# A four-layer attention kernel on one Trainium2 core: row maxima transposed before they are split, and the layer norm's pieces spread between them

## The reference, cut to what matters

```python
x = L0_attn_a_x                                             # (16, 512, 256), fp32
x = x + _L0_attn_a_ref(_layernorm(x, axis=-1), ...)         # causal
x = x + _L0_ffn_ref(_layernorm(x, axis=-1), ...)            # split
x = x + _L0_attn_b_ref(_layernorm(x, axis=-1), ...)         # rotary
x = x + _L0_ffn_ref(_layernorm(x, axis=-1), ...)            # split
# inside each: scores = q k^T / sqrt(16); attn = softmax(scores); out = attn v; out @ Wo
```

## Time and profile before

| what | value |
|---|---|
| median of 3 runs | 4944.91 us (4940.63 to 4948.76) |
| the profiled execution: its own time | 4945.49 us |
| the profiled execution: span of its trace | 4943.7 us |
| mean granted TensorE clock in the span | 0.974 |
| PE busy | 4445.3 us, 90% |
| DVE busy | 3209.4 us, 65% |
| ACT busy | 2548.2 us, 52% |
| POOL busy | 1656.7 us, 34% |

### The profile page before, as it was taken

How to read it: one execution, slowest core, us unless ns; L and a number is a source line. 1 busy time by engine, 2 the same in 40 slices (tenths; PEclk the granted TensorE clock), 3 DMA queues, 4 the chain that set the end, 5 groups by cost and what they waited for, 6 DMA issues and landing times.

```text
span 4943.7 us, 70632 instructions
## 1 busy us (share of the span) xinstructions
PE 4445.3 (90%) x26116; PEld 1877.8 (38%) x26116; DVE 3209.4 (65%) x6576; ACT 2548.2 (52%) x3362; POOL 1656.7 (34%) x922
## 2 busy tenths in 40 slices
PE   4899999999969999899898999999999699999998
PEld 2454545454423333333333333333333233333333
DVE  4555555555447776767676676676676277777776
ACT  1444444444425555555455555555555255666565
POOL 2354545454432344352534334334324400000000
PEclk8999999999979999999999999999999799999999
DMA  4453535344322333423333334334333133333331
GB/s 131 122 155 118 156 114 156 124 150 127 107 89 82 92 114 96 114 83 113 99 96 112 98 113 120 96 106 120 98 104 120 54 86 90 89 89 90 91 89 44
DMA packets 302406, 525.36 MB, mean 106 GB/s; under 512 B 58348, under 2 KB 236272, under 8 KB 285680
## 3 DMA queue, kind: packets, MB, share of 16 engines
q1 hardware_dynamic: 259568, 485.19, 33.7%
q10 hardware_dynamic: 42496, 35.66, 2.2%
HBM read 317.10 MB, written 201.46 MB: 105 GB/s over the span
## 4 chain that ended last, share of the span: by engine, by line
PE 71%; DVE 17%; DMA 6%; issue 3%; ACT 3%; POOL 1%; DVEq 0%; ACTq 0%; SPq 0%; POOLq 0%
PE o_ps L1249 17%; PE scores L1197 16%; PE scores_t L1228 11%; DVE neg_max L864 10%; PE turn_ps L1277 10%; DMA q_stack<-shift_rows 5%; PE turn_ps L1324 5%; PE turn_ps L1284 4%; PE turn_ps L1255 4%; DVE bn L822 2%; DVE xn L839 2%; PE turn_ps L1289 1%; DVE shift_parts L874 1%; PE scores L1200 1%; PE scores L1212 1%
## 5 line engine op out<-in xcount | busy, mean ns | idle before, releaser
L864 DVE TENSOR_REDUCE neg_max<-scores 128x1 f32<-128x512 f32 (+3 forms) x4096 | 2489.2, 636 | 1285.9 <-PE scores L1197 760.0
L1065 ACT ACTIVATE probs<-scores_t 128x1024 f32<-128x1024 f32 (+2 forms) x2048 | 1926.3, 947 | 1484.8 <-PE scores_t L1228 1007.3
L1197 PE MATMUL scores<-k_stack,q_stack 98*128 98x512 bf16 (+4 forms) x4096 | 1428.3, 371 | 239.6 <-DVE neg_max L864 179.5
L1228 PE MATMUL scores_t<-q_stack,k_stack 100*128 100x512 bf16 (+3 forms) x4096 | 1187.5, 364 | 59.2 <-DMA q_stack<-shift_rows 58.3
L1249 PE MATMUL o_ps<-probs,values 128*32 128x512 f32 (+1 forms) x8192 | 1021.4, 571 | 0.2 <-ACT probs L1065 0.2
L1197 PEld LDWEIGHTS scores<-k_stack,q_stack 96*128 96x128 bf16 (+1 forms) x4096 | 396.7, 97 | 1635.8 <-DVE neg_max L864 1209.1
L1228 PEld LDWEIGHTS scores_t<-q_stack,k_stack 100*128 100x128 bf16 x4096 | 378.4, 99 | 380.5 <-issue 137.7
L725 POOL TENSOR_TENSOR parts<-qk_f,parts 128x1024 bf16<-128x1024 f32 x128 | 272.6, 2130 | 660.3 <-ACT parts L1105 491.1
L745 POOL TENSOR_TENSOR sim_inv<-sim_parts,minus_half 128x64 f32<-128x64 f32 x32 | 337.7, 10552 | 249.9 <-DVE sim_parts L946 249.9
L738 POOL TENSOR_TENSOR x_res<-x_res,o_bias_s 128x1024 f32<-128x1024 f32 x32 | 75.6, 2362 | 956.8 <-DMA x_res<-x_after 956.8
L696 POOL TENSOR_SCALAR var_eps<-mean_var 128x4 f32<-128x4 f32 x64 | 14.7, 230 | 978.6 <-DVE mean_var L828 978.6
(11 more groups left out here) (117 smaller groups left out, 4035.2 us busy)
## 6 DMA issues: line engine op xcount, KB each, us to landing
q_stack<-q_parts SPq DMA_DIRECT2D x1536, 64.0 KB, 2.6
values<-v_stage SPq DMA_DIRECT2D x64, 1024.0 KB, 4.2
values<-values SPq DMA_DIRECT2D x64, 1024.0 KB, 6.2
k_parts<-parts SPq DMA_DIRECT2D x192, 256.0 KB, 2.7
q_parts<-parts SPq DMA_DIRECT2D x192, 256.0 KB, 3.3
k_stack<-k_parts SPq DMA_DIRECT2D x256, 192.0 KB, 3.2
k_stack<-k_parts SPq DMA_DIRECT2D x256, 128.0 KB, 3.2
x_after<-x_res ACTq DMA_DIRECT2D x48, 512.0 KB, 2.9
```

The costliest lines, as they stand in the source:

```text
L864: nc.vector.tensor_reduce(neg_max[:, h % G, t:t + 1], bank[:, 0:n], AX.X, ALU.max, negate=True).then_inc(max_done.sem, 1)
L1065: nc.scalar.activation(probs[c][:, h % G, 0:n], st[i][:, 0:n], ACT.Exp).then_inc(exp_done.sem, 1)
L1197: last = nc.tensor.matmul(bank[:, 0:n], q[0:r, h, t * P:(t + 1) * P], k[0:r, h, 0:n], start=True, stop=kind != CAUSAL)
L1228: last = nc.tensor.matmul(st[i][:, off:off + L - q0], k[0:ROWS, h, kt * P:(kt + 1) * P], q[0:ROWS, h, q0:L], start=True, stop=kind != CAUSAL)
```

## The change

Three things are changed.

1. The maxima are not split before the transpose. PE transposes the 16 columns of `neg_max` as fp32 (16 by 128 in PSUM); DVE then makes the high part by a cast from PSUM and the low part by a subtraction whose first operand is in PSUM and whose second is the high part in SBUF. `shift` and `shift_parts` are gone. `neg_max` has two halves, used by groups in turn.
2. ACT issues two transfers for a group, one for each row of `q_stack`, from 16 partitions each.
3. Statistics and normalisation are cut into single pieces, one behind each maximum: the next stage's statistics at (slot, tile) (6,0), (6,2), (6,3), (7,0), the four BN_AGGR at (7,1), the normalisation at (8,0) to (8,3). The later batch's are at (9,0) to (9,3), (10,0), and (11,0) to (11,3).

```diff
-NXT_STATS_AT = (6, 1)
-NXT_NORMALISE_AT = (8, 0)
-X_STATS_AT = (8, 1)
-X_NORMALISE_AT = (10, 1)
+NXT_STATS_AT = {(6, 0): 0, (6, 2): 1, (6, 3): 2, (7, 0): 3, (7, 1): T}
+NXT_NORMALISE_AT = {(8, t): t for t in range(T)}
+X_STATS_AT = {(9, 0): 0, (9, 1): 1, (9, 2): 2, (9, 3): 3, (10, 0): T}
+X_NORMALISE_AT = {(11, t): t for t in range(T)}
...
-        neg_max = sb("neg_max", [P, G, T])
-        shift_parts = sb("shift_parts", [P, 2, G * T], BF16)
-        shift_rows = sb("shift_rows", [2 * G * T, P], BF16)
+        neg_max = sb("neg_max", [P, 2, G, T])
+        shift_rows = sb("shift_rows", [G * T, 2, P], BF16)
...
             def maximum(B, h, t):
                 kind = STAGES[B.s]
 
-                if h % G == 0 and t == 0 and (h or not B.first):
-                    shift_ready.wait(dve, B + (0 if h else -1), (h // G - 1) % NG)
+                g = h // G
+                if h % G == 0 and t == 0 and (g >= 2 or not B.first):
+
+                    turn_full.wait(dve, B + (0 if g >= 2 else -1), "sh", (g - 2) % NG)
...
-            def shift(B, g):
-
-                dve.wait_ge(max_done.sem, max_done.after(B, G * g + G - 1, T - 1))
-
-                if g or not B.first:
-                    turn_full.wait(dve, B + (0 if g else -1), "sh", (g - 1) % NG)
-                nm = neg_max[:, :, :].rearrange("p h t -> p (h t)")
-                nc.vector.tensor_copy(shift_parts[:, 0, :], nm).then_inc(shift_high.sem, 1)
-                dve.wait_ge(shift_high.sem, shift_high.after(B, g))
-                nc.vector.tensor_tensor(shift_parts[:, 1, :], nm, shift_parts[:, 0, :],
-                                        ALU.subtract).then_inc(shift_ready.sem, 1)
...
-                    nc.vector.tensor_copy(shift_rows[:, :], turn_b[0:2 * G * T, :]).then_inc(turn_free.sem, 1)
+                    rows = turn_ps[0:G * T, 0:P]
+                    nc.vector.tensor_copy(shift_rows[:, 0, :], rows).then_inc(shift_high.sem, 1)
+                    dve.wait_ge(shift_high.sem, shift_high.after(B, i))
+                    nc.vector.tensor_tensor(shift_rows[:, 1, :], rows, shift_rows[:, 0, :],
+                                            ALU.subtract).then_inc(turn_free.sem, 1)
...
-                act.dma_start(q_stack[B.n % 2][SHIFT:SHIFT + 2, G * g:G * g + G, :],
-                              shift_rows[:, :]).then_inc(shift_in.sem, 16)
+                for a in range(2):
+                    act.dma_start(q_stack[B.n % 2][SHIFT + a:SHIFT + a + 1, G * g:G * g + G, :],
+                                  shift_rows[:, a, :]).then_inc(shift_in.sem, 16)
...
                 elif k == "sh":
-                    pe.wait_ge(shift_ready.sem, shift_ready.after(B, i))
+                    pe.wait_ge(max_done.sem, max_done.after(B, G * i + G - 1, T - 1))
...
                 elif k == "sh":
-                    last = nc.tensor.transpose(turn_b[0:2 * G * T, :],
-                                               shift_parts[:, :, :].rearrange("p a c -> p (a c)"), ident_b[:, :])
+                    last = nc.tensor.transpose(turn_ps[0:G * T, 0:P],
+                                               neg_max[:, i % 2, :, :].rearrange("p h t -> p (h t)"), ident[:, :])
```

104 lines of the change are left out of this document (52 added, 52 removed).

## The result

| what | before | after |
|---|---|---|
| median of 4 runs | 4946.84 us | 5061.16 us (5046.37 to 5072.54) |
| ratio, 95% interval | | 1.0228 (1.0195 to 1.0262) |
| the profiled execution: time, span | 4945.49, 4943.7 us | 5054.6, 5052.8 us |
| mean granted clock | 0.974 | 0.967 |
| PE busy | 4445.3 us | 4496.3 us |

What follows compares the result with a forecast made beforehand. PE was taken to set the end, standing where it waits for DVE's maxima, statistics and normalisation and for the shift's transfer. Terms -66 - 55 - 40 + 22 + 15 + 0 = -124 from 4945.5 us gave 4820, range 4755 to 4900.

Steps and rivals of the forecast that it cites:

- Stalls behind POOL: Shift instructions with both ends in SBUF, which wait for POOL, are removed, mainly in the split stage's slot 2: -66 us.
- Single pieces: Statistics and normalisation between maxima in slots 6 to 11 hold PE up less: -55 us, between 15 and 91 gained.
- The pair in slots 1, 5, 9, 13 is gone: Without DVE's split ahead of the transpose, 0.5 us returns in 80 slots of the later stages: -40 us.
- The fp32 transpose: Each of PE's 256 shift transposes takes 0.28 us instead of 0.23: +15 us with the longer weight load.
- The pair behind the transpose: Cast and subtraction, 0.4 us longer than one copy, delay the first maximum of slots 3, 7, 11, 15: +22 us.
- Two transfers: Landing of the shift's rows: later and earlier effects of two requests cancel: 0 us, between -50 and +75.
- "earlier" side: For the rows' landing: a shorter issue, 0.42 us for 0.62, and 0.65 us less queueing bring 0.85 us.
- "later" side: For the rows' landing: 0.4 us for DVE and 0.42 for the second issue delay it by 0.82 us.
- "Slower": Rival: both transfers queue like the worst seen, one behind the other, rows landing 2.5 us later: 5070 us, chance 0.05.
- The gain of about 35 us: By the skill's rule a one-row transfer runs on 16 engines instead of 2, making the time about 35 us lower.

Runs made afterwards that it cites:

- a_runs: The changed kernel with one three-row transfer in place of two of one row, and statistics and normalisation in runs as before; 5019 us, ratio 1.0128.
- b_ kernels: Variants of the kernel before; the five meant keep its old cast and subtraction and edit only transfers or SP's store; 4870 to 5111 us.
- b_pieces: The kernel before with only statistics and normalisation cut into single pieces between the maxima; 4870 us, ratio 0.9833.
- b_two: The kernel before with only the transfer changed: two transfers of one row in place of one of two rows; 5111 us, ratio 1.0327.
- a_one: The changed kernel with one transfer of three rows, the middle one zeros, in place of two of one row; 4926 us, ratio 0.9955.
- b_halves: The kernel before with two transfers of two rows and two heads each, cut by heads instead of by rows; 5043 us, ratio 1.0170.
- b_high: The kernel before with one transfer of one row, the low row left out and staying zero; 4934 us, ratio 0.9971.
- a_early: The changed kernel with the shift's turn at place 0 of its slot and both transfers issued behind that slot's second exponential; 4729 us, ratio 0.9550.
- a_hold_late: The changed kernel with the shift's turn at place 0, both transfers issued in the next slot, also behind its first maximum on DVE; 5160 us, ratio 1.0424.

## Why the prediction was wrong

**Stalls behind POOL (-66), right.** No cast or subtraction is above 0.28 us; a slot 2 of the split stage lasts 3.5 us (median), and slot 2 of the split stage is 53 us shorter in all, where the prediction's terms make 50 (43 for the double stalls, 8 for the pair, less 1 for the transposes). The waits for maxima fell by 45 us in a_runs. What the term did not say is that its size hangs on the moment: in five of the b_ kernels 31 to 40 us of it went without any edit to the pair.

**Single pieces (-55, between 15 and 91), right in kind, low in size:** 83 and 93 measured. The causal stage gave what was taken for it (-42 us in slots 7, 9, 10 and 11 of b_pieces, for 35), the split and the rotary stage about twice (-39 for 20). Where a rotary batch waited 1.22 us in slot 7 and 0.35 in slot 8 or 9, one of the changed kernel waits for maxima 0.21 us twice and 0.35 once in slots 7 to 9.

**The pair in slots 1, 5, 9, 13 is gone (-40), right:** slot 2 of the last stage, 3.89 us in before's batch above (4269.77 to 4273.66), is 3.48 after (4360.26 to 4363.74); 0.41 with the longer transpose in it, for the 0.5 forecast without.

**The fp32 transpose (+15), right:** 256 instructions of 275 ns against 233 in the earlier trace rows, 11 us.

**The pair behind the transpose (+22), the first failing step.** Its length was right (0.58 us for 0.20), but it was priced only at "the first maximum of slots 3, 7, 11 and 15". What stands behind it is ACT's request, which leaves 0.52 us later, and PE's `og` transposes, which need the bank. The stalls, the pair, the transpose and this term were to bring 69 us together; with one request, a_runs lost 63. The table by slots parts the two sides: up to the transpose (slots 2, 6, 10 and 14) a_runs gained 128 us, more than the 91 of the three other terms, and in the slots behind it (15, 0, 3, 4, 7, 8, 9, 11) it lost 206, where the forecast had 22. A three-row request with an issue of 0.73 us is part of that, how large a part is not shown.

**Two transfers (0, between -50 and +75), the step that decided.** Measured 162 in b_two, and 135 between a_one and the change. The working gave an "earlier" side of 0.85 us, mostly "less queueing, since each carries half the packets". The "later" side was right (0.52 us for DVE and 0.54 for the second issue, for 0.4 and 0.42); the relief that was to cancel it did not come. The second request is not half of one place in the queues but a second place, and what SP has issued up to then stands ahead of it: in the split stage the store, 0.11 us behind the first request, in slot 3, by the timeline alone, the loads. The kernel before already showed such a collision, with a single request: in the instance of the earlier trace rows with 5.09 us the store is issued 0.12 us behind it. Reading SP's queue in that window would have shown what arrives in the half microsecond that a second issue takes. The rival "Slower" (each queues like the worst, one behind the other, 2.5 us later, 5070), given 0.05, had the mechanism, and in the split stage the size: the second wave lands 2.5 us behind the first. That its time is off by only 9 us is in part luck: it took 250 us more of waits for the rows, where 139 came, and had neither the bank's 53 nor PE's slower products in its sum.

The packets did spread: 50176 on ACT's queue, 7680 more than in the earlier trace rows, which is 256 x 30, a completion from 16 engines for each of two requests where two completed before. The Trainium skill, "DMA: Bandwidth & Descriptors", section "Why a DMA increments its semaphore by 16 and not by 1", is borne out by that count. Two more counts agree: b_halves has 43008, 512 more than before, which is two completions for each of two requests, and a_one 46848, 4352 more, which is 16 rows and one completion more for each group. The gain of about 35 us worked out beside it did not come. One spread request gained nothing outside slot 2 of the split stage (b_high), and two spread requests are 68 us slower than two narrow ones (b_two, b_halves).

**Idle was counted one for one.** Between before and after PE's three waits grow by 69 us, the time by 114. PE's busy time grew by 51 us with as many instructions; 11 us of that are the transposes'. Per stage (window, length, PE busy, ..., clock), the rotary stage before and after:

```profile
2689.90:3959.30 1269.40, 1148.00 (x5726) 442.90 (x5726) 841.35 (x1619) 699.52 (x893) 454.43 (x249) 0.97 0.35 104
```

```profile
2712.00:4040.70 1328.70, 1179.14 (x5726) 447.47 (x5726) 805.92 (x1556) 699.25 (x893) 454.03 (x249) 0.95 0.34 99
```

The same 5726 instructions take 31 us more at a mean granted clock of 0.95. Over the kernels of the table, the highest clock (0.984) stands beside 55 us of these waits and the lowest (0.952) beside 348, but the clock does not follow their sum alone: b_two has the most (365) at 0.967. A microsecond of PE's waits comes with more than one of time: (5160 - 4729) / (347.6 - 55.3) = 1.5 between a_early and a_hold_late, (5111 - 4947) / (364.7 - 237.8) = 1.3 for b_two, 114 / 69 = 1.7 for the change. What of the extra is the clock's was not measured by itself.

## What to carry to other kernels

Before changing how a small transfer is made, measure its slack from the event that issues it to the instruction that awaits it, and add the whole delay of the new chain (every instruction ahead of the request, and the second issue). Where there is no slack (here in two of a batch's four groups), each tenth of a microsecond is paid in full, and PE's products were slower on top. A second request is a second place in the queues: look in the other queues for what is issued between the two or just ahead of them, and either hold that back or move the small transfer half a step earlier, where how it is made no longer matters. When a variant is timed, look also at places that it does not touch: here a stall that came and went there was worth 31 to 40 us, more than some of the edits. A change that loses as it is (the split behind the transpose) may be what makes the better order possible: 5061 became 4729 by moving the turn it had set free.

## What was not expected of the hardware

A 4 KB request of ACT issued 0.4 us behind a 1 MB store of SP landed 4.5 us after its issue, the one issued 0.11 us ahead of that store after 2.6, and one alone takes 1.6 to 2. A kernel with its shift cut by heads was 68 us faster than one with it cut by rows (b_halves, b_two), with the same landing in the slot where the store falls between the requests (PE starts 5.25 us behind the first issue, 1709.34 to 1714.59, against 5.11). The difference lies almost all in slots 15 and 0 (50 us against 107), and there mostly in the causal and the rotary stage, where the store is issued 2.1 us ahead of both: in the rotary stage PE starts 4.3 us (median) behind the first issue with two engines for each request and 5.2 with 16. Why wide requests suffer more behind the store than narrow ones is not shown.
